# The three bf16 parts of q and k written to DRAM and loaded back one by one, and value products, projection and output normalization shifted by one unit

## The reference

```python
y = jnp.mean(x, axis=(2, 3)); y = conv1d(y, w_c)
yc = sigmoid(x * y)                                  # channel gate
sa = sigmoid(conv2d(concat(mean_c(yc), max_c(yc)), w_s))
x = yc * sa + x                                      # spatial gate
xn = groupnorm(x, 32 groups) * gn_w + gn_b
q, k, v = split(einsum('bchw,oc->bohw', xn, qkv_w) + qkv_b)
attn = softmax(einsum('bndi,bndj->bnij', q, k) / 4)  # 4 heads, 256 x 256
out = einsum('bnij,bndj->bndi', attn, v)
return x + einsum('bchw,oc->bohw', out, proj_w) + proj_b
```

## Time and profile before

| what | us |
|---|---|
| median of 3 runs | 199.0 (196.49 to 199.06) |
| profiled execution | 195.77 |
| its span | 193.9 |
| TensorE busy | 168.6 (87%) |
| VectorE busy | 142.1 (73%) |
| ScalarE busy | 122.6 (63%) |
| GpSimd busy | 112.2 (58%) |
| packets of the main DMA queue, share of 16 engines' span | 51.1% |

### The profile page before, as it was taken

One profiled execution on the slowest core, in us unless ns is written; L12 is line 12 of the kernel. 1 busy time (PEld: TensorE's weight loads), 2 busy tenths in 40 slices (PEclk: granted clock), 3 DMA queues, 4 the chain that ended last, 5 costly groups with the idle time before them and its releaser, 6 DMA issues.

```text
span 193.9 us, 4752 instructions
## 1 busy us (share of the span) xinstructions
PE 168.6 (87%) x1515; PEld 105.4 (54%) x1518; DVE 142.1 (73%) x295; ACT 122.6 (63%) x250; POOL 112.2 (58%) x214
## 2 busy tenths in 40 slices
PE   7698985986959999989999998999999898888881
PEld 2265674453546667565656666576666655453320
DVE  0947769256743998888989897897989679797353
ACT  3073540451537797968878696977879686657760
POOL 5991282858473948678686968679784370101110
PEclk9969999999996999999999999999999999999999
DMA  3940302779397684637485755736676574600011
GB/s 100 358 111 19 108 3 83 167 221 210 84 227 163 165 202 122 158 119 167 148 172 144 194 126 145 162 124 148 194 177 129 154 163 125 176 28 3 28 32 54
DMA packets 19558, 26.24 MB, mean 135 GB/s; under 512 B 3756, under 2 KB 16468, under 8 KB 19540
## 3 DMA queue, kind: packets, MB, share of 16 engines
q1 hardware_dynamic: 18960, 25.47, 51.1%
q10 hardware_dynamic: 580, 0.55, 1.1%
HBM read 17.35 MB, written 8.42 MB: 133 GB/s over the span
## 4 chain that ended last, share of the span: by engine, by line
PE 34%; DMA 23%; SPq 20%; DVE 7%; POOL 6%; ACT 5%; issue 5%; POOLq 0%; ACTq 0%
DMA ks<-parts_dram 18%; SPq L256 11%; PE bank L667 7%; PE bank L693 7%; SPq L257 6%; PE bank L679 5%; PE bank L703 3%; DMA parts_dram<-parts 3%; PE bank L606 3%; DVE negmax L546 2%; SPq L244 2%; ACT pt L408 2%; PE bank L722 2%; DMA con<-consts 2%; PE bank L713 1%
## 5 line engine op out<-in xcount | busy, mean ns | idle before, releaser
L546 DVE TENSOR_REDUCE negmax<-bank 128x2 bf16<-128x512 f32 x128 | 86.1, 683 | 27.4 <-PE bank L667 24.9
L408 ACT ACTIVATE pt<-bank 128x512 f32<-128x512 f32 x128 | 73.5, 592 | 19.1 <-PE bank L679 18.9
L667 PE MATMUL bank<-ks,qs 96*128 96x256 bf16 x256 | 49.9, 276 | 11.3 <-DMA ks<-parts_dram 8.9
L679 PE MATMUL bank<-qs,ks 97*128 97x256 bf16 x256 | 49.2, 274 | 2.1 <-ACT pt L408 2.0
L667 PEld LDWEIGHTS bank<-ks,qs 96*128 96x128 bf16 x256 | 20.5, 101 | 38.5 <-DVE negmax L546 23.6
L693 PE MATMUL bank<-pt,vs 128*32 128x256 f32 x512 | 34.0, 383 | 0.1
L333 POOL TENSOR_TENSOR rest<-z,parts 128x512 f32<-128x512 f32 x15 | 17.4, 1158 | 27.5 <-ACT z L417 14.8
L679 PEld LDWEIGHTS bank<-qs,ks 97*128 97x128 bf16 x256 | 24.3, 98 | 8.2 <-ACT pt L408 4.6
L306 POOL TENSOR_TENSOR xall<-yo,xall 128x256 f32 (+1 forms) x15 | 10.9, 726 | 26.0 <-ACT yo L428 25.9
L693 PEld LDWEIGHTS bank<-pt,vs 128*32 128x32 f32 x512 | 14.8, 110 | 12.3 <-issue 3.4
L703 PE MATMUL bank<-xn,wall 128*128 128x256 f32 x64 | 20.0, 400 | 1.0 <-ACT xn L400 0.9
(11 more groups left out here) (70 smaller groups left out, 216.1 us busy)
## 6 DMA issues: line engine op xcount, KB each, us to landing
parts_dram<-parts SPq DMA_DIRECT2D x16, 384.0 KB, 2.6
qs<-parts_dram SPq DMA_DIRECT2D x16, 192.0 KB, 3.7
ks<-parts_dram SPq DMA_DIRECT2D x16, 192.0 KB, 4.0
xall<-x SPq DMA_DIRECT2D x4, 512.0 KB, 5.9
qs<-parts_dram SPq DMA_DIRECT2D x16, 128.0 KB, 3.9
ks<-parts_dram SPq DMA_DIRECT2D x16, 128.0 KB, 3.8
out<-xall SPq DMA_DIRECT2D x16, 128.0 KB, 2.2
gate<-gate_dram SPq DMA_DIRECT2D x6, 256.0 KB, 4.1
```

The costliest lines, as they stand in the source:

```text
L408: nc.scalar.activation(pt[:, (u + LEAD) % UNITS, :, :].rearrange("p t n -> p (t n)"), st_bank[u % 2][:, :], ACT.Exp, scale=SCALE).then_inc ...
L546: nc.vector.tensor_reduce(negmax[:, slot(1), column:column + TILES], s_bank[u % 2][:, :].rearrange("p (t n) -> p t n", t=TILES), AX.X, ALU ...
L667: mm = pe.matmul(s_bank[u % 2][:, t * N:(t + 1) * N], qs[0:KQ, slot(1), h, a, t * P:(t + 1) * P], ks[0:KQ, slot(1), h, a, :], start=True, ...
L679: mm = pe.matmul(st_bank[u % 2][:, t * N:(t + 1) * N], ks[0:KQ + 1, slot(d), h, a, t * P:(t + 1) * P], qs[0:KQ + 1, slot(d), h, a, :], sta ...
```

## The change

SP writes each part on its own: part 0 as soon as ScalarE has made it, part 1 after GpSimd's copy, part 2 after the subtraction, each with a semaphore of its own (`parts_out[0..2]`). The store of the output stands between the first and the second write. It reads them back in seven DMAs in place of six: three for part 0 ahead of the wait for `maxrow`, two for part 1 and two for part 2 behind the `maxrow` DMA. The six slots hold the same six products in another order. GpSimd waits for `st_ready` (the fourth st of the turn) before it computes part 2. On VectorE the reciprocal goes from u = 0 to u = 1, the product from u = 1 to u = 2 ahead of the transpose, and `gn_group` goes behind the maximum of u = 7. On TensorE proj and pv(1) go from u = 5 to u = 4.

```diff
--- before.py
+++ after.py
@@ -155,7 +155,7 @@
         z_ready, v_ready = sem("z_ready"), sem("v_ready")
         p1_ready, z32_ready = sem("p1_ready"), sem("z32_ready")
         split_step = sem("split_step")
-        parts_out, stack_in = sem("parts_out"), [sem(f"stack_in{r}") for r in range(RING)]
+        parts_out, stack_in = [sem(f"parts_out{i}") for i in range(3)], [sem(f"stack_in{r}") for r in range(RING)]
         s_ready, max_done = sem("s_ready"), sem("max_done")
         mt_ready, mrow_ready, mrow_in = sem("mt_ready"), sem("mrow_ready"), sem("mrow_in")
         st_ready, exp_done = sem("st_ready"), sem("exp_done")
@@ -239,29 +239,37 @@
             aside = {(0, 2): lambda: gate_read(sp, 2), (1, 2): lambda: gate_read(sp, 3)}
             def turn(k, slot, has, lap):
+                def stack(tile, g, part, first, copies):
+
+                    r = slot(2)
+                    rows = slice(first * HD, (first + copies) * HD)
+                    src = parts_dram[r, part, g, :, :].unsqueeze(0).broadcast_to([copies, HD, HEADS * 2 * N])
+                    sp.dma_start(tile[rows, r, :, :, :].rearrange("p h a n -> p (h a n)"), src).then_inc(stack_in[r], 16)
+
+                def part_write(part):
+                    r = slot(3)
+                    sp.dma_start(parts_dram[r, part].rearrange("g d (h n) -> (g d h) n", h=HEADS),
+                                 parts[:, r, part, :]).then_inc(parts_out[part], 16)
+
+                if has(2):
+                    wait(sp, parts_out[0], 16 * (k + 3))
+                    stack(qs, 0, 0, 0, 3)
+                    stack(ks, 1, 0, 1, 1)
+                    stack(ks, 1, 0, 4, 2)
                 if has(0):
                     wait(sp, mrow_ready, k + 1)
                     sp.dma_start(qs[KQ:KQ + 1, slot(0), :, :, :].rearrange("p h a (t n) -> p (h a t) n", t=TILES),
                                  maxrow[:, slot(0), :]).then_inc(mrow_in, 16)
-
-
                 if has(2):
-                    r = slot(2)
-                    wait(sp, parts_out, 16 * (k + 3))
-                    for first, q_parts, k_part in ((0, 3, 0), (3, 2, 1), (5, 1, 2)):
-
-                        rows = slice(first * HD, (first + q_parts) * HD)
-                        src_q = parts_dram[r, 0:q_parts, 0, :, :].rearrange("s d n -> d s n")
-                        src_k = parts_dram[r, k_part, 1, :, :].unsqueeze(1).broadcast_to([HD, q_parts, HEADS * 2 * N])
-                        sp.dma_start(qs[rows, r, :, :, :].rearrange("p h a n -> p (h a n)"), src_q).then_inc(stack_in[r], 16)
-                        sp.dma_start(ks[rows, r, :, :, :].rearrange("p h a n -> p (h a n)"), src_k).then_inc(stack_in[r], 16)
-
-
+                    wait(sp, parts_out[1], 16 * (k + 3))
+                    stack(qs, 0, 1, 3, 2)
+                    stack(ks, 1, 1, 2, 2)
+                    wait(sp, parts_out[2], 16 * (k + 3))
+                    stack(qs, 0, 2, 5, 1)
+                    stack(ks, 1, 2, 0, 1)
                 if has(3):
-                    r = slot(3)
-                    wait(sp, split_step, 3 * (k + 4))
-                    sp.dma_start(parts_dram[r].rearrange("s g d (h n) -> (g d h) s n", h=HEADS), parts[:, r, :, :]).then_inc(parts_out, 16)
-
+                    wait(sp, p1_ready, k + 4)
+                    part_write(0)
                 if has(-3):
                     wait(sp, out_ready, k - 2)
                     if isinstance(k, int):
@@ -269,6 +277,11 @@
                     else:
                         dst = out[bass.ds(2 * (k - 3), 2)].rearrange("i c n -> (i c) n")
                     sp.dma_start(dst, at(xall, k - 3)).then_inc(stored, 16)
+                if has(3):
+                    wait(sp, split_step, 3 * (k + 3) + 2)
+                    part_write(1)
+                    wait(sp, split_step, 3 * (k + 4))
+                    part_write(2)
                 stands_in(aside, k, 2)
             pipeline(sp, turn)
             sp.wait_ge(out_ready, PAIRS)
@@ -343,6 +356,7 @@
                     nc.gpsimd.tensor_tensor(gnb[:, :], gnm[:, :], b_gn, ALU.add).then_inc(gn_shift, 1)
                 if on_pool:
                     nc.gpsimd.tensor_scalar(parts[:, r, 1, :], rest[:, :], 1.0, 0.0, ALU.mult, ALU.add).then_inc(split_step, 1)
+                    wait(pool, st_ready, UNITS * k)
                     wait(pool, split_step, 3 * (k + 3) + 2)
                     nc.gpsimd.tensor_tensor(parts[:, r, 2, :], rest[:, :], parts[:, r, 1, :], ALU.subtract).then_inc(split_step, 1)
             pipeline(pool, turn)
@@ -410,7 +424,7 @@
                     if u == 0 and has(3):
                         wait(act, z_ready, k + 4)
-                        wait(act, parts_out, 16 * k)
+                        wait(act, parts_out[0], 16 * k)
                         nc.scalar.activation(parts[:, slot(3), 0, :], z_bank[:, :], ACT.Identity, bias=b_qk).then_inc(p1_ready, 1)
                     if u == 1 and has(3):
                         wait(act, split_step, 3 * (k + 2) + 1)
@@ -533,8 +547,6 @@
                 for u in range(UNITS):
                     stands_in(aside, k, u)
-                    if u == 7 and has(5):
-                        gn_group()
                     if u == 4 and has(5):
                         wait(dve, gn_stat, 2 * (k + 5) + 1)
                         wait(dve, gs_ready, k + 5)
@@ -546,8 +558,11 @@
                         nc.vector.tensor_reduce(negmax[:, slot(1), column:column + TILES],
                                                 s_bank[u % 2][:, :].rearrange("p (t n) -> p t n", t=TILES),
                                                 AX.X, ALU.max, negate=True).then_inc(max_done, 1)
-                    if u <= 2 and has(-2):
-                        norm(u + 1, -2, 1 if last(-2) else None)
+                    if u == 7 and has(5):
+                        gn_group()
+                    for i in {1: (1,), 2: (2, 3)}.get(u, ()):
+                        if has(-2):
+                            norm(i, -2, 1 if last(-2) else None)
                     if u == 2 and isinstance(k, int) and k + 3 == 0:
                         dve.wait_ge(p1_ready, 1)
@@ -662,7 +677,7 @@
                     a, h = u // HEADS, u % HEADS
                     wait(pe, max_done, UNITS * (k + 1) + u - 1)
                     if u == 0:
-                        wait(pe, stack_in[slot(1)], lap(1) * 96)
+                        wait(pe, stack_in[slot(1)], lap(1) * 112)
                     for t in range(TILES):
                         mm = pe.matmul(s_bank[u % 2][:, t * N:(t + 1) * N], qs[0:KQ, slot(1), h, a, t * P:(t + 1) * P],
                                        ks[0:KQ, slot(1), h, a, :], start=True, stop=True)
@@ -758,9 +773,9 @@
                         v()
                     if u == 2 and has(-1):
                         pv(0)
-                    if u == 5 and has(-2):
+                    if u == 4 and has(-2):
                         proj()
-                    if u == 5 and has(-1):
+                    if u == 4 and has(-1):
                         pv(1)
                     if u == 6 and has(5):
                         groupstats()
```

## The result

The changed kernel took 302.31 us (297.87 to 303.83) against 198.05 for the kernel before: ratio 1.514, interval 1.488 to 1.540. The prediction said 188, range 183 to 196. It is wrong by far, and on the other side.

What follows compares the result with a forecast made beforehand. Two close bounds were named: the loop through the reads (up to 8.9 us a turn) and TensorE's order (8.27). Terms -3.0, -3.6, -2.5, -0.3 gave -9.4: 186.4 profiled, 189.6 from the median; 188.0 forecast, range 183 to 196.

Steps and rivals of the forecast that it cites:

- Landing in 3.4 to 4.0 it is there at T'+7.3 to 7.9: SP's last read, issued at T'+3.9 (T' starts the next turn), lands ahead of T'+8.05, so reads leave the path.
- A wait put at nothing: On SP, after part 2's write (0.45), three reads of part 0 follow at 0.62 each; SP is free at T+9.4.
- The third rival: Maxima's DMA behind 384 KB of reads takes 3.9 and becomes the loop: turns of 9.25, 205 us; chance 0.08.
- The second rival: Reads land no earlier because DMA engines, busy share 0.62, set the pace: only the start gains, -2, 196.5 us; chance 0.12.
- The sum itself: All terms over the whole kernel: -9.4 us against the profiled 195.77, so 186.4 for that execution.
- until turn 3: Start-up: earlier part writes and reads gain before turn 3, less a cost in turn 1: -3.0 us.
- turns 3 to 10: Eight steady turns shorten from 8.61 to 8.15 us each: -3.6 us.
- turns 11 to 13: Three late turns, where TensorE has less to do, shorten from 8.55 to 7.7 us each: -2.5 us.
- the rest: Turn 14 gains -0.3 us; the end behind it 0.
- The maxima's wait: st(4) waiting for the maxima's DMA: 0.1 us per steady turn, from nothing to 0.7; in turn 1 some 2 us.
- the 4.6 us that SP is said to have spent on the maxima and the six reads: SP's issue time per turn before the change, used to claim it has room for 0.6 + 0.9 us more.
- The first rival: The shift on TensorE gives nothing, another wait replacing the 0.28 us, while reads leave the path: turns 8.35, 192 us; chance 0.18.

Runs made afterwards that it cites:

- e1: The kernel before with only the dimension order of its six reads changed, copies outermost, then the 16 rows: 329.55 us, ratio 1.678.
- e2: The changed kernel with each copy read by a DMA of its own, 12 reads of 64 KB in place of 7: 202.97 us, ratio 1.032.
- e5: The changed kernel with six spread reads (16 rows outermost), slots ordered as in the kernel before but split by part: 188.04 us, ratio 0.948.
- e3: The changed kernel with the maxima's DMA issued ahead of the three reads of part 0, copies still outermost: 328.9 us, ratio 1.683.
- e6: e5 with the TensorE and VectorE part of the change undone: 189.45 us, ratio 0.948.
- e10: e5 with the gate reads of turns 0 and 1 moved from the turn's end to behind the reads of part 2: 190.32 us, ratio 0.969.
- e11: e6 with the gate reads of turns 0 and 1 moved from the turn's end to behind the reads of part 2: 192.16 us, ratio 0.984.
- e4: The kernel before with copies outermost in its two reads of 48 rows only: 265.23 us, ratio 1.357.

## Why the prediction was wrong

- **The step that failed** is "Landing in 3.4 to 4.0 it is there at T'+7.3 to 7.9". That landing was taken from the earlier trace rows, whose reads had the 16 rows outermost. The new reads have the copies outermost, and the prediction treated their count and bytes as all that had changed. e1 shows that this one swap costs 132 us on the kernel before (329.55 to 197.53), and e2 and e5 that the rest of the change doesn't cost it. In place of 3.4 to 4.0 the last read took 10.92 in e1. In the changed kernel, whose reads show no landing, everything behind them was late: the maxima took 7.2 for 1.7, the writes 9.3 for 2.6. SP issued the maxima in time (at 157.08, 1.95 into its turn); it was the landing that failed. The rule on the number of engines stands in the same page of the Trainium skill that the prediction cited for another, and would have warned ahead.
- **A wait put at nothing.** The prediction let SP go from the write of part 2 straight to the three reads of part 0. They wait for the write of part 0 to land, and SP stood 104.0 us for that, 15 times. With spread reads the same wait is small: in e5 the writes land in 2.2, and SP stood 4.0 us for them in all.
- **The third rival** (the maxima's DMA becomes the loop) named the right place: st(4) waited 61.9 us for it. Its price was capped by the landing of a large read, 3.9; it measured 7.2, and the writes 9.3, which no rival had. Its mechanism, large reads ahead on the queue, says where the wait stands and not why the time is lost: e3 has none ahead, its maxima land in 1.7, and it took 328.9.
- **The second rival** asked whether the DMA engines set the pace and looked at their mean share, 0.62. The mean can't answer it: in the changed kernel it fell, while the engines of the narrow reads were the pace.
- **The sum itself** came near, for a change that spreads its reads: e5 has six of them with 256 KB ahead of the maxima, where the sum was made for seven with 384 KB. Seven spread reads in the change's own order were not run. e5's own execution took 188.23, 7.5 less than 195.77, where the sum said 9.4. By its terms: until turn 3 (s(0) at 73.87 for 75.52) -1.7 for -3.0, because of the three waits for the maxima; turns 3 to 10 -5.0 for -3.6 (7.98 a turn, s(0) of turn 11 at 137.72, for 8.15); turns 11 to 13 (turn 14 at 161.42) -2.0 for -2.5; the rest +1.1 for -0.3, at a lower clock. No term is right to a tenth and the errors have both signs, so the median that falls on 188.0 owes that to chance.
- **The maxima's wait** in a steady turn was put at 0.1; e5 has none there. In turn 1 it was put at 2 us; e5 has 1.39 there, 1.07 and 1.37 on the turns beside it.
- **A reading that was off:** the 4.6 us that SP is said to have spent on the maxima and the six reads is 4.2 by the earlier trace rows (128.67 to 132.88). It changed nothing in the sum.
- **The first rival** (the shift gives nothing) is refuted for the turn (7.95 against 8.25) and open for the whole (e5 and e6 alike, e10 and e11 0.015 apart).

## What to carry to other kernels

A DMA is priced by how its rows are dealt to the DMA engines before its bytes are counted: look at the outermost dimension of both access patterns in every line that a change rewrites, and keep a multiple of 16 there; a broadcast over copies goes inside. A duration from a trace holds for the access pattern that was timed and not for its size. Where DMAs get late while the mean share of the DMA engines falls, look for a flat stretch in a table of windows: 2/16 or 3/16 is an engine count.

## What I had not expected of the hardware

- Narrow reads delay what stands behind them on the queue, also DMAs that are spread themselves: in e1 a spread read of 64 KB landed after 10.92 us, in the changed kernel 4 KB of maxima after 7.2.
- A single DMA engine moved some 25 GB/s here (49 to 53 GB/s at a share of 0.12 to 0.13; in e4 three moved 66 at a share of 0.19, some 22 each).
- Waiting was paid twice: when TensorE went on after 5.6 us without work the granted clock was 0.50 for the next 6 us, and the mean over the span was 0.81 against 0.98 before.
- SP's issue alone fills a turn of 8.42 us with 12 reads, the maxima, three writes and a store (e2): more and smaller DMAs have a price even where they are all spread.
